# An attention and ternary-FFN kernel: scores issued one block ahead, half of a quantisation moved to ScalarE

## The chip, the cores and the metric

The kernel runs on all 8 cores of one Trainium2 chip, each core on one of the 8 sequences of the batch, with no exchange between them. The metric is the device time in microseconds of the slowest core. A core has TensorE (matmuls, results in PSUM), VectorE (DVE), ScalarE (ACT), GpSimd (POOL) and SyncE (SP); each works through its own queue in order and meets the others at semaphores. TensorE's clock is granted at one of two levels, 1.2 or 2.4 GHz; a granted clock of 0.67 over a stretch is a mean of 0.5 (1.2 GHz) and 1.0 (2.4 GHz).

## The reference

Per sequence (T = 2048 rows, C = 1024 columns, 16 heads of 64, hidden width 4096). What matters of it:

```
xn   = layernorm(x)
attn = softmax(q @ k.T / 8) @ v,  q, k, v = xn @ w{q,k,v}.T + b
y    = attn @ wo.T + bo
xq   = round(xn * 127/max|xn|) / (127/max|xn|)       # act_quant, per row
wq   = clip(round(w / mean|w|), -1, 1) * mean|w|     # weight_quant
h    = silu(depthwise_conv3(xq @ w1q.T) + conv_b)
out  = x + y + act_quant(h) @ w2q.T
```

Heads take 64 columns each; a key whose first input is 0 is masked.

## The kernel before

Five stages follow each other, written out as one queue per engine; nothing but the order of the code sets the order of the work.

**Layer norm (to about 240 us), L162 to L313.** 16 tiles of 128 rows. For each tile VectorE reduces, ScalarE squares (L217) and takes a square root (L226), VectorE normalises into `xn_t` (L279), casts to `xnb_t`, finds the maximum and quantises into `xqb_t`: L300 multiplies by the scale, L303 adds and subtracts `meff` (the constant that rounds), L306 multiplies back. TensorE transposes both (L185) through `psB`, and `evac` copies them to `xnT` and `xqT`. Between these, ScalarE streams the 64 chunks of the two FFN weights through `wf` to sum their absolute values: `wabs` (L206) frees a slot, `wdma` (L199) then issues the load of the chunk two ahead, so two loads of 512 KB are in flight.

**Projections (to about 316 us), L573.** q and k of the first pair of heads and v of the first four heads, from `xnT`, into `psD`, copied out by VectorE (L647, L653).

**Attention (316 to 1785 us), L576 to L595 and L605 to L624.** 8 pairs of heads, 4 blocks of 512 queries, 16 blocks of 128 keys: 512 blocks j. `scores(j)` (L564, L567, one head on each half of the rows) writes 1024 columns into half j%2 of `psA`. ScalarE takes the exponential into one of three slots of `probs` (L617). `emit_ctx(j)` (L537, L541) multiplies `probs` by v and accumulates in `psC`; its extra column of ones gives the denominators. After 16 blocks VectorE copies sums and denominators out (L683 to L687), TensorE spreads the denominators over partitions (L551, L553) and VectorE takes the reciprocal (L661) and scales. A second stream fills the gaps: the projections of the next heads, in halves of four matmuls, one half at every even block in the first six pairs of heads (q and k in the first 32 blocks, v in the other 32), at every fourth block in the seventh, none in the eighth. A third stream quantises the FFN weights: per 8 blocks one load (L380), two ScalarE operations (L387, L395), a clip on VectorE (L638) and a store (L413).

TensorE's queue goes by pairs of blocks: the context of the pair before, two projection slots, then the scores of both blocks. The first score of the pair waits until the exponentials of the pair before are done (L591), since they read the halves of `psA` that it writes.

**Output projection, L702 to L741.** GpSimd loads `wo_bf` over the memory of `xnT`, `wf`, `wqb`, `wblk` and `wvq` once these are free (its waits are L703 to L706); TensorE waits for that load at L716.

**FFN (to the end)**: first matmul, convolution, silu, row maximum, quantisation, second matmul, by blocks of 512 rows. The change does not touch it.

Of the kernel before, what the change touches and what calls it, by code (L numbers as in the profile page):

```python
# [11 lines left out]
AF = mybir.ActivationFunctionType  # L12
# [3 lines left out]
NT = T // 128  # L16
# [17 lines left out]
def _build():  # L34
# [24 lines left out]
    def sem(name):  # L59
        if name not in semn:  # L60
            semn[name] = E(nc.semaphore(name))
            cnt[name] = 0
        return semn[name]
# [51 lines left out]
    def on(engname, fn):  # L115
        getattr(blk, engname)(fn)
# [75 lines left out]
    def p1_scalar(s):  # L192
# [10 lines left out]
        def wabs(ch):  # L203
# [5 lines left out]
            inc("wabs")  # L209

        wdma(0); wdma(1)
        for i in range(NT):
            b = i % 2
# [7 lines left out]
            for ch in (4 * i, 4 * i + 1):  # L221
                wabs(ch)
                if ch + 2 < NW:
                    wdma(ch + 2)
            s.wait_ge(sem("p1v"), 18 * i + 5)
            s.activation(out=stt[:, b * 16 + 3:b * 16 + 4],  # L226
# [3 lines left out]
            for ch in (4 * i + 2, 4 * i + 3):  # L230
                wabs(ch)
                if ch + 2 < NW:
                    wdma(ch + 2)
    on("scalar", p1_scalar)

    def p1_vector(v):
# [14 lines left out]
        for i in range(NT):  # L251
# [25 lines left out]
            v.tensor_tensor(c(7), c(6), c(5), OP.mult).then_inc(sem("p1v"), 1); inc("p1v")  # L277
            v.wait_ge(sem("p1v"), val("p1v"))
            v.tensor_scalar(xnt, xt, c(1), c(7), OP.add, OP.mult).then_inc(  # L279
                sem(f"xf{b}"), 1)  # L280
# [4 lines left out]
            if i >= 2:  # L285
# [13 lines left out]
            v.wait_ge(sem("p1v"), val("p1v"))  # L299
            v.tensor_scalar(xnt, xnt, c(11), None, OP.mult).then_inc(sem("p1v"), 1); inc("p1v")  # L300
            v.wait_ge(sem("p1v"), val("p1v"))
            v.wait_ge(sem("p0v"), MEFF)
            v.tensor_scalar(xnt, xnt, meff[:, 0:1], meff[:, 0:1],  # L303
                            OP.add, OP.subtract).then_inc(sem("p1v"), 1); inc("p1v")
            v.wait_ge(sem("p1v"), val("p1v"))
            v.tensor_scalar(xqb_t[:, b * 1024:(b + 1) * 1024], xnt,  # L306
                            invsx[:, i:i + 1], None, OP.mult).then_inc(sem("p1xq"), 1); inc("p1xq")
            if i >= 1:
# [176 lines left out]
    def p23_tensor(t):  # L485
# [71 lines left out]

        def scores(j):
            it, kc = divmod(j, NT)
            hp, qb = divmod(it, NQB)  # L560
            pp = kc % 2
            sA = psA[:, pp * 1024:pp * 1024 + 512]
            sB = psA[:, pp * 1024 + 512:pp * 1024 + 1024]
            t.matmul(sA, kTv[0:64, hp % 2, kc * 128:(kc + 1) * 128],  # L564
                     qTv[0:64, hp % 2, qb * 512:(qb + 1) * 512],
# [5 lines left out]
            inc("p3s")  # L571

        for item in prods[:PROLOG]:  # L573
            prod_block(item)
        NJ3 = NHP * NQB * NT
        for pm in range(NJ3 // 2):  # L576
            j0 = 2 * pm
            it, kc = divmod(j0, NT)
            hp, qb = divmod(it, NQB)
            jl0 = j0 - hp * 64  # L580
            if jl0 == 0:
                t.wait_ge(sem("pde"), last_k[hp] + 1)
            if j0 >= 2:
                emit_ctx(j0 - 2)
                emit_ctx(j0 - 1)
            for item, half in seg_sched[hp].get(jl0, []):
                prod_block(item, half)
            for item, half in seg_sched[hp].get(jl0 + 1, []):
                prod_block(item, half)
            if j0 >= 2:  # L590
                t.wait_ge(sem("p3exp"), j0)  # L591
            scores(j0)
            scores(j0 + 1)
        emit_ctx(NJ3 - 2)
        emit_ctx(NJ3 - 1)  # L595
# [106 lines left out]
    def p35_gload(g):  # L702
        g.wait_ge(sem("p3pf"), P3PF)  # L703
        g.wait_ge(sem("wqv"), NW)
# [534 lines left out]
```

## Time and profile before

| what | us |
|---|---|
| median of 3 runs | 2784.5 (2782.46 to 2786.21) |
| profiled execution | 2784.95 |
| its span (slowest core, core 4) | 2783.3 |
| spans of the 8 cores | 2753.5 to 2783.3 |
| TensorE matmul busy | 1686.4 (61%) |
| ScalarE busy | 1118.1 (40%) |
| VectorE busy | 968.4 (35%) |
| GpSimd busy | 101.6 (4%) |

No engine is busy for most of the span. The busy time is a mean over stages with different limits, so each stage is read by itself: a table by stretches says where an engine is full and at which clock, and the timeline of a stretch says who waited for whom. In a timeline row the bracket at the end is the idle time of that engine just before the row, and what ended it. Matmuls overlap in their pipeline, so the distance between two starts tells more than the duration of one.

### The profile page before, as it was taken

The numbers are of one execution on the slowest core, as the hardware profiler recorded it, in microseconds if no ns is written. First come the engines' busy times: TensorE is split into PE (matmuls) and PEld (weight loads), VectorE is DVE, ScalarE is ACT, GpSimd is POOL, SyncE is SP. The second block draws the span as 40 slices with busy tenths as digits, with TensorE's granted clock in tenths as the row PEclk, the third lists the DMA queues.
The fourth block names the chain that finished last, engine by engine and source line by source line (L and its number), as shares of the span: only waits on it lengthen the run. The fifth ranks groups of instructions, "written<-read, shape, count | busy, mean of one in ns | idle before, by whom it ended". The sixth has DMA issues, their size and how long they took to land.

```text
span 2783.3 us, 24362 instructions; the slowest of 8 cores (2753.5 to 2783.3 us)
## 1 busy us (share of the span) xinstructions
PE 1686.4 (61%) x6887; PEld 571.6 (21%) x6986; DVE 968.4 (35%) x1392; ACT 1118.1 (40%) x1331; POOL 101.6 (4%) x193
## 2 busy tenths in 40 slices
PE   0114666666666666666666666398656666676666
PEld 0112211111111111111111111033323232232222
DVE  5674122221212121212112221213678258348423
ACT  3441244444444444443444455302356036126215
POOL 0000000000000000000000000000111001001000
PEclk9999576676665867767656655589888888888889
DMA  6754021111111111111100010201221422432344
GB/s 167 199 196 106 7 46 35 37 38 35 37 43 34 38 38 36 41 35 38 38 34 34 35 38 34 39 15 41 70 76 65 127 89 66 131 97 66 115 120 143
DMA packets 117954, 186.33 MB, mean 67 GB/s; under 512 B 44482, under 2 KB 77379, under 8 KB 117828
## 3 DMA queue, kind: packets, MB, share of 16 engines
q10 hardware_dynamic: 36864, 83.90, 10.0%
q0 software_dynamic: 16864, 50.35, 6.8%
q1 hardware_dynamic: 64100, 50.52, 6.1%
q8 instruction: 64, 1.05, 0.1%
q14 instruction: 62, 0.51, 0.1%
HBM read 167.95 MB, written 25.17 MB: 69 GB/s over the span
## 4 chain that ended last, share of the span: by engine, by line
PE 45%; ACT 17%; issue 13%; DMA 12%; DVE 11%; ACTq 1%; DVEq 0%; SPq 0%; POOL 0%; POOLq 0%
ACT probs L617 11%; PE psC L537 7%; PE psD L501 6%; DMA wf<-w_t 6%; PE psA L564 5%; PE psC L541 5%; PE psA L867 5%; PE psC L914 4%; PE psD L513 4%; DVE amax L1039 3%; ACT wf L387 3%; DMA w2q_sb<-w2q_stage 3%; PE psA L725 2%; PE psC L551 2%; DVE u_sb L1058 1%
## 5 line engine op out<-in xcount | busy, mean ns | idle before, releaser
L617 ACT ACTIVATE probs<-psA,bias_exp 128x1024 bf16<-128x1024 f32 x512 | 548.8, 1110 | 782.1 <-PE psA L567 782.0
L537 PE MATMUL psC<-probs,vroll 128*65 128x512 bf16 x512 | 256.5, 501 | 427.3 <-ACT probs L617 427.3
L867 PE MATMUL psA<-xqT,w1q_sb 128*128 128x512 bf16 x984 | 289.5, 440 | 159.6 <-DVE u_sb L1063 94.8
L541 PE MATMUL psC<-probs,vroll 128*65 128x512 bf16 x512 | 267.6, 523 | 0.0
L567 PE MATMUL psA<-qroll,kroll 64*128 64x512 bf16 x512 | 227.8, 540 | 0.0
L564 PE MATMUL psA<-qroll,kroll 64*128 64x512 bf16 x512 | 227.5, 539 | 0.0
L537 PEld LDWEIGHTS psC<-probs,vroll 128*65 128x65 bf16 x512 | 61.5, 120 | 778.7 <-issue 778.7
L914 PE MATMUL psC<-w2q_sb,hq 128*128 128x512 bf16 x561 | 162.7, 400 | 72.4 <-DMA w2q_sb<-w2q_stage 42.1
L501 PE MATMUL psD<-xnT,wblk 128*128 128x512 bf16 x480 | 185.2, 521 | 18.7 <-issue 5.6
L777 ACT ACTIVATE u_sb<-psA,cws 128x512 f32<-128x512 f32 x128 | 87.1, 681 | 262.8 <-PE psA L872 262.4
L799 ACT ACTIVATE qscr<-qscr,meff 128x512 f32<-128x512 f32 x128 | 91.5, 715 | 226.8 <-DVE qscr L1074 214.0
L647 DVE CAST vroll<-psD 128x256 bf16<-128x256 f32 x64 | 27.3, 427 | 439.1 <-PE psD L520 439.1
L867 PEld LDWEIGHTS psA<-xqT,w1q_sb 128*128 128x128 bf16 x1024 | 101.5, 107 | 285.2 <-issue 217.9
L513 PE MATMUL psD<-wvq,xnT 128*128 128x256 bf16 x512 | 121.8, 393 | 13.3 <-DVE vroll L647 12.2
L1058 DVE SCALAR_TENSOR_TENSOR u_sb<-psA,cws,u_sb 128x512 f32<-128x512 f32 x128 | 95.8, 749 | 90.8 <-ACT u_sb L777 90.8
L653 DVE TENSOR_SCALAR qroll<-psD,bqc 128x512 bf16<-128x512 f32 x32 | 24.0, 751 | 284.5 <-PE psD L501 284.5
L551 PE MATMUL psC<-denrow,onesr_s 1*64 1x512 f32 x64 | 60.2, 1042 | 96.5 <-DVE denrow L687 96.5
L185 PE MATMUL psB<-identb_s,xqb_t 128*128 128x128 bf16 x128 | 16.2, 307 | 168.9 <-DVE xnT L247 168.9
L653 DVE TENSOR_SCALAR kroll<-psD,bkc 128x512 bf16<-128x512 f32 x32 | 24.0, 751 | 266.0 <-PE psD L501 266.0
L661 DVE RECIPROCAL rtile<-psC 128x512 f32<-128x512 f32 x32 | 107.2, 3349 | 9.3 <-PE psC L553 9.2
L206 ACT ACTIVATE wf<-wf 128x1024 f32<-128x1024 f32 x64 | 67.6, 1056 | 99.9 <-DMA wf<-w_t 96.3
L1039 DVE TENSOR_REDUCE amax<-h_act 128x512 f32<-128x2048 f32 x28 | 102.9, 3676 | 5.7 <-ACT h_act L788 5.7
(139 smaller groups left out, 1999.3 us busy)
## 6 DMA issues: line engine op xcount, KB each, us to landing
wf<-w_t ACTq DMA_DIRECT2D x128, 512.0 KB, 4.1
w1q_sb<-w1q_stage POOLq DMA_DIRECT2D x128, 256.0 KB, 2.9
w2q_sb<-w2q_stage SPq DMA_DIRECT2D x128, 128.0 KB, 2.2
w2q_sb<-w2q_stage ACTq DMA_DIRECT2D x128, 128.0 KB, 2.2
x_t<-x SPq DMA_DIRECT2D x16, 512.0 KB, 7.2
w1q_stage<-wqb SPq DMA_DIRECT2D x32, 256.0 KB, 2.5
w2q_stage<-wqb SPq DMA_DIRECT2D x32, 256.0 KB, 2.0
xr_t<-x POOLq DMA_DIRECT2D x32, 256.0 KB, 3.8
```

The source lines that it names most:

```text
L501: mm = t.matmul(psD[:, 0:512], wblk[:, off + cc * 128:off + (cc + 1) * 128], xnTv[:, cc, b * 512:(b + 1) * 512], start=(cc == 0), stop=(cc ...
L513: t.matmul(psD[:, 0:256], xnTv[:, cc, ti * 128:(ti + 1) * 128], wvq[:, (qv % 2) * 2048 + cc * 256:(qv % 2) * 2048 + (cc + 1) * 256], start ...
L537: t.matmul(psC[0:65, 0:512], v_v[:, qvj % 2, kcj, laj, 0:65], probs[:, pslot * 1024:pslot * 1024 + 512], start=(kcj == 0), stop=(kcj == NT ...
L541: mm = t.matmul(psC[0:65, 512:1024], v_v[:, qvj % 2, kcj, laj + 1, 0:65], probs[:, pslot * 1024 + 512:pslot * 1024 + 1024], start=(kcj == ...
L551: t.matmul(psC[0:64, 1024:1536], onesr[0:1, 0:64], denrow[0:1, 0:512], start=True, stop=True)
L564: t.matmul(sA, kTv[0:64, hp % 2, kc * 128:(kc + 1) * 128], qTv[0:64, hp % 2, qb * 512:(qb + 1) * 512], start=True, stop=True, tile_positio ...
L567: mm = t.matmul(sB, kTv[64:128, hp % 2, kc * 128:(kc + 1) * 128], qTv[64:128, hp % 2, qb * 512:(qb + 1) * 512], start=True, stop=True, til ...
L617: s.activation(out=probs[:, pslot * 1024:(pslot + 1) * 1024], in_=psA[:, pp * 1024:(pp + 1) * 1024], func=AF.Exp, scale=0.125, bias=bias_e ...
L867: t.matmul(ps[:, 0:512], w1q_sb[:, b * 1024 + cc * 128:b * 1024 + (cc + 1) * 128], xqTv[:, cc, tb * 512:tb * 512 + 512], start=(cc == 0), ...
L914: mm = t.matmul(psm2, hq_v[:, jc, tt * 128:(tt + 1) * 128], w2q_sb[:, b2 * 512:(b2 + 1) * 512], start=(jc == 0), stop=(jc == NJC - 1))
L1039: v.reduce_max(amax2[:], hT[:, :, 4 * k:4 * k + 4], axis=AX, apply_absolute_value=True).then_inc(sem("p4fo"), 1)
L1058: v.scalar_tensor_tensor(u_sb[:, ub * 512:(ub + 1) * 512], ps[:, 1:513], cws[:, jc * 3 + 1:jc * 3 + 2], u_sb[:, ub * 512:(ub + 1) * 512], ...
```

## The change

Three edits, the instructions of which are otherwise the same.

**Attention.** TensorE's queue goes block by block: scores of block j, context of block j-1, the projection slot of block j. The wait for the exponential that frees the half of `psA` is now for block j-2 alone.

**Layer norm.** VectorE multiplies by the scale and adds `meff` in one operation (L300 and the addition of L303). The subtraction and the multiplication back become two ScalarE operations, in `quant_tail`, placed for tile i-1 after the second weight chunk of tile i and ahead of its square root; the last tile's stand at the end. VectorE's count of `p1v` per tile falls from 18 to 16.

**wo load.** Its wait for the last context matmul becomes one for the last q, k and v projections; the waits for the quantised weights and their stores stay.

```diff
+        def quant_tail(i2):
+            b2 = i2 % 2
+            xnt2 = xn_t[:, b2 * 1024:(b2 + 1) * 1024]
+            s.wait_ge(sem("p1q1"), i2 + 1)
+            s.activation(out=xnt2, in_=xnt2, func=AF.Identity,
+                         bias=meffneg[:, 0:1]).then_inc(sem("p1rt"), 1)
+            s.wait_ge(sem("p1rt"), val("p1rt"))
+            if i2 >= 2:
+                s.wait_ge(sem("p1tpm"), 2 * i2 - 2)
+            s.activation(out=xqb_t[:, b2 * 1024:(b2 + 1) * 1024], in_=xnt2,
+                         func=AF.Identity,
+                         scale=invsx[:, i2:i2 + 1]).then_inc(sem("p1xq"), 1)
...
+            if i >= 1:
+                quant_tail(i - 1)
+            s.wait_ge(sem("p1v"), 16 * i + 5)
-            s.wait_ge(sem("p1v"), 18 * i + 5)
...
+            if i >= 2:
+                v.wait_ge(sem("p1xq"), i - 1)
             v.tensor_scalar(xnt, xt, c(1), c(7), OP.add, OP.mult).then_inc(
...
-            v.tensor_scalar(xnt, xnt, c(11), None, OP.mult)
-            v.tensor_scalar(xnt, xnt, meff[:, 0:1], meff[:, 0:1],
-                            OP.add, OP.subtract)
-            v.tensor_scalar(xqb_t[:, b * 1024:(b + 1) * 1024], xnt,
-                            invsx[:, i:i + 1], None, OP.mult)
+            v.tensor_scalar(xnt, xnt, c(11), meff[:, 0:1],
+                            OP.mult, OP.add).then_inc(sem("p1q1"), 1)
...
-        for pm in range(NJ3 // 2):
-            j0 = 2 * pm
-            if j0 >= 2:
-                emit_ctx(j0 - 2)
-                emit_ctx(j0 - 1)
-            for item, half in seg_sched[hp].get(jl0, []): ...
-            for item, half in seg_sched[hp].get(jl0 + 1, []): ...
-            if j0 >= 2:
-                t.wait_ge(sem("p3exp"), j0)
-            scores(j0)
-            scores(j0 + 1)
+        for j in range(NJ3):
+            if j >= 2:
+                t.wait_ge(sem("p3exp"), j - 1)
+            scores of block j, as before
+            if j >= 1:
+                emit_ctx(j - 1)
+            for item, half in seg_sched[hp].get(jl, []):
+                prod_block(item, half)
...
     def p35_gload(g):
-        g.wait_ge(sem("p3pf"), P3PF)
+        g.wait_ge(sem("qkp"), 8 * NHP)
+        g.wait_ge(sem("vmm"), 4 * NT)
```

TensorE's queue before, at the end of the first 16 blocks. L564 and L567 are scores, L537 and L541 context, L551 and L553 the spread denominators, L501 a projection half:

```order
L564 MATMUL psA<-qroll,kroll 128x512 [waits p3exp]
L567 MATMUL psA<-qroll,kroll 128x512
L564 MATMUL psA<-qroll,kroll 128x512
L567 MATMUL psA<-qroll,kroll 128x512
L537 MATMUL psC<-probs,vroll 65x512 [waits p3exp,pde]
L541 MATMUL psC<-probs,vroll 65x512
L537 MATMUL psC<-probs,vroll 65x512 [waits p3exp,pde]
L541 MATMUL psC<-probs,vroll 65x512
L551 MATMUL psC<-denrow,onesr_s 64x512 [waits p3ev2]
L553 MATMUL psC<-denrow,onesr_s 64x512
L501 MATMUL psD<-xnT,wblk 128x512 [waits pde,lk]
L501 MATMUL psD<-xnT,wblk 128x512 x3
```

The same place after, where L588 and L591 are scores, L553 and L557 context, L567 and L569 the denominators and L517 the projection half:

```order
L588 MATMUL psA<-qroll,kroll 128x512 [waits p3exp]
L591 MATMUL psA<-qroll,kroll 128x512
L553 MATMUL psC<-probs,vroll 65x512 [waits p3exp,pde]
L557 MATMUL psC<-probs,vroll 65x512
L588 MATMUL psA<-qroll,kroll 128x512 [waits p3exp]
L591 MATMUL psA<-qroll,kroll 128x512
L553 MATMUL psC<-probs,vroll 65x512 [waits p3exp,pde]
L557 MATMUL psC<-probs,vroll 65x512
L567 MATMUL psC<-denrow,onesr_s 64x512 [waits p3ev2]
L569 MATMUL psC<-denrow,onesr_s 64x512
L517 MATMUL psD<-xnT,wblk 128x512 [waits pde,lk]
L517 MATMUL psD<-xnT,wblk 128x512 x3
```

One block's scores now stand between two blocks' contexts, so the scores of the first block of the next 16 are ahead of the last context and of the denominators; the projection half and the scores after it still stand behind the denominators.

ScalarE's queue in layer norm before, from the second weight chunk of a tile on (L206 weight chunk, L199 the load two ahead, L226 square root):

```order
L206 ACTIVATE wf,wsum<-wf 128x1024 [waits wl2]
L199 DMA wf<-w_t 128x1024 [waits wabs]
L226 ACTIVATE stt<-stt 128x1 [waits p1v]
L206 ACTIVATE wf,wsum<-wf 128x1024 [waits wl0]
L199 DMA wf<-w_t 128x1024 [waits wabs]
```

And after, where L244 is the square root and L215 and L221 are `quant_tail`:

```order
L206 ACTIVATE wf,wsum<-wf 128x1024 [waits wl2]
L199 DMA wf<-w_t 128x1024 [waits wabs]
L215 ACTIVATE xn_t<-xn_t,meffneg 128x1024 [waits p1q1]
L221 ACTIVATE xqb_t<-xn_t,invsx 128x1024 [waits p1rt]
L244 ACTIVATE stt<-stt 128x1 [waits p1v]
L206 ACTIVATE wf,wsum<-wf 128x1024 [waits wl0]
L199 DMA wf<-w_t 128x1024 [waits wabs]
```

Two operations of 128x1024 now stand ahead of the square root and of the third weight chunk of each tile but the first.

## Rows read from the trace of the kernel before

**Rows 1.** The page's costliest groups; count, busy us, mean ns, idle before and releaser.
```profile
L617 ACT ACTIVATE probs<-psA,bias_exp 128x1024 bf16<-128x1024 f32 x512 | 548.8, 1110 | 782.1 <-PE psA L567 782.0
...
L537 PE MATMUL psC<-probs,vroll 128*65 128x512 bf16 x512 | 256.5, 501 | 427.3 <-ACT probs L617 427.3
...
L661 DVE RECIPROCAL rtile<-psC 128x512 f32<-128x512 f32 x32 | 107.2, 3349 | 9.3 <-PE psC L553 9.2
```

**Rows 2.** Stretches: length, PE, PEld, DVE, ACT, POOL busy, clock, DMA share, GB/s.
```profile
0.00:240.00 240.00, 33.17 (x263) 25.54 (x263) 152.30 (x381) 96.24 (x177) 2.85 (x9) 1.00 0.62 176
...
316.00:1785.00 1469.00, 939.08 (x3021) 237.90 (x3048) 306.62 (x325) 682.27 (x641) 7.41 (x14) 0.67 0.13 36
...
1800.00:2000.00 200.00, 156.48 (x709) 61.42 (x725) 79.46 (x91) 32.44 (x49) 13.48 (x26) 0.88 0.17 45
```

**Rows 3.** Timeline, last pair of heads, 1.2 GHz; start, duration, engine, line, idle before.
```profile
1757.54 0.60 PE L564 MATMUL psA<-qroll,kroll 64*128 64x512 bf16 x1
...
1758.30 2.12 ACT L617 ACTIVATE probs<-psA,bias_exp 128x1024 bf16<-128x1024 f32 x2 [1.98 <-PE psA L567]
...
1759.67 0.60 PE L537 MATMUL psC<-probs,vroll 128*65 128x512 bf16 x1 [1.09 <-ACT probs L617]
...
1760.67 0.61 PE L537 MATMUL psC<-probs,vroll 128*65 128x512 bf16 x1
...
1761.64 0.60 PE L564 MATMUL psA<-qroll,kroll 64*128 64x512 bf16 x1
```

**Rows 4.** Timeline, a pair with half a k product, 2.4 GHz.
```profile
568.43 2.12 ACT L617 ACTIVATE probs<-psA,bias_exp 128x1024 bf16<-128x1024 f32 x2 [3.55 <-PE psA L567]
...
570.80 0.38 PE L537 MATMUL psC<-probs,vroll 128*65 128x512 bf16 x1 [0.41 <-ACT probs L617]
...
572.18 0.39 PE L564 MATMUL psA<-qroll,kroll 64*128 64x512 bf16 x1
...
572.73 1.11 ACT L617 ACTIVATE probs<-psA,bias_exp 128x1024 bf16<-128x1024 f32 x1 [1.15 <-PE psA L567]
```

**Rows 5.** Timeline, TensorE, 1.2 GHz: with half a v, and half a k product.
```profile
447.90 0.61 PE L537 MATMUL psC<-probs,vroll 128*65 128x512 bf16 x1
...
450.04 0.60 PE L564 MATMUL psA<-qroll,kroll 64*128 64x512 bf16 x1
...
565.13 0.61 PE L537 MATMUL psC<-probs,vroll 128*65 128x512 bf16 x1 [1.54 <-ACT probs L617]
...
567.80 0.46 PE L564 MATMUL psA<-qroll,kroll 64*128 64x512 bf16 x1
```

**Rows 6.** Timeline, the accumulators emptied after 16 blocks, 1.2 GHz.
```profile
1741.92 0.61 PE L537 MATMUL psC<-probs,vroll 128*65 128x512 bf16 x1
...
1744.84 1.22 DVE L687 COPY denrow<-psC 1x1024 f32<-1x1024 f32 x1
...
1746.31 1.08 PE L551 MATMUL psC<-denrow,onesr_s 1*64 1x512 f32 x1 [3.36 <-DVE denrow L687]
...
1748.21 0.60 PE L564 MATMUL psA<-qroll,kroll 64*128 64x512 bf16 x1
```

**Rows 7.** Layer norm: waits to 215 us, then timeline of one tile.
```profile
ACT wf L206 <- DMA wf<-w_t: 92.5, 51, 3.9
...
197.38 0.20 ACT L226 ACTIVATE stt<-stt 128x1 f32<-128x1 f32 x1 [0.51 <-DVE stt L267]
...
199.15 1.06 ACT L206 ACTIVATE wf<-wf 128x1024 f32<-128x1024 f32 x1 [1.57 <-DMA wf<-w_t]
...
204.66 0.75 DVE L306 TENSOR_SCALAR xqb_t<-xn_t,invsx 128x1024 bf16<-128x1024 f32 x1
```

**Rows 8.** Groups in attention, shapes apart; count, busy us, mean ns.
```profile
L395 ACT ACTIVATE wf<-wf,meffneg 128x1024 f32<-128x1024 f32 x64 | 73.3, 1146 | 0.0
```

**Rows 9.** Timeline after the last exponential, GpSimd.
```profile
1794.73 4.23 POOL L708 DMA_DIRECT2D wo_bf<-wo_t  x8 [447.45 <-DMA w2q_stage<-wqb]
```

**Rows 10.** Line 617: duration in ns, least, median and most; first and last start.
```profile
L617 ACT ACTIVATE probs<-psA,bias_exp x512: 1100/1112/1116, 317.6 to 1779.5; 128x1024 bf16<-128x1024 f32 x171
```

More of the change, by code:

```diff
@@ L209, in wabs @@
             inc("wabs")
+        def quant_tail(i2):
[4 more added lines that the diff above has]
+                         bias=meffneg[:, 0:1]).then_inc(sem("p1rt"), 1)
+            inc("p1rt")
+            s.wait_ge(sem("p1rt"), val("p1rt"))
[4 more added lines that the diff above has]
+                         scale=invsx[:, i2:i2 + 1]).then_inc(sem("p1xq"), 1)
+            inc("p1xq")
         wdma(0); wdma(1)
+        s.wait_ge(sem("p0v"), MEFF)
         for i in range(NT):
@@ L233, in p1_scalar @@
                     wdma(ch + 2)
+        quant_tail(NT - 1)
     on("scalar", p1_scalar)
@@ L299, in p1_vector @@
             v.wait_ge(sem("p1v"), val("p1v"))
-            v.tensor_scalar(xnt, xnt, c(11), None, OP.mult).then_inc(sem("p1v"), 1); inc("p1v")
-            v.wait_ge(sem("p1v"), val("p1v"))
             v.wait_ge(sem("p0v"), MEFF)
-            v.tensor_scalar(xnt, xnt, meff[:, 0:1], meff[:, 0:1],
-                            OP.add, OP.subtract).then_inc(sem("p1v"), 1); inc("p1v")
-            v.wait_ge(sem("p1v"), val("p1v"))
-            v.tensor_scalar(xqb_t[:, b * 1024:(b + 1) * 1024], xnt,
-                            invsx[:, i:i + 1], None, OP.mult).then_inc(sem("p1xq"), 1); inc("p1xq")
+            v.tensor_scalar(xnt, xnt, c(11), meff[:, 0:1],
+                            OP.mult, OP.add).then_inc(sem("p1q1"), 1); inc("p1q1")
             if i >= 1:
@@ L556, in emit_ctx @@
                 inc("p3nb")
-        def scores(j):
+        for item in prods[:PROLOG]:
+            prod_block(item)
+        NJ3 = NHP * NQB * NT
+        for j in range(NJ3):
             it, kc = divmod(j, NT)
             hp, qb = divmod(it, NQB)
+            jl = j - hp * 64
+            if jl == 0:
+                t.wait_ge(sem("pde"), last_k[hp] + 1)
             pp = kc % 2
@@ L571, in scores @@
             inc("p3s")
-        for item in prods[:PROLOG]:
-            prod_block(item)
-        NJ3 = NHP * NQB * NT
-        for pm in range(NJ3 // 2):
-            j0 = 2 * pm
[L578 to L582, printed above, removed]
-            if j0 >= 2:
-                emit_ctx(j0 - 2)
-                emit_ctx(j0 - 1)
-            for item, half in seg_sched[hp].get(jl0, []):
-                prod_block(item, half)
-            for item, half in seg_sched[hp].get(jl0 + 1, []):
-                prod_block(item, half)
-            if j0 >= 2:
-                t.wait_ge(sem("p3exp"), j0)
-            scores(j0)
-            scores(j0 + 1)
-        emit_ctx(NJ3 - 2)
+            if j >= 1:
+                emit_ctx(j - 1)
+            for item, half in seg_sched[hp].get(jl, []):
+                prod_block(item, half)
         emit_ctx(NJ3 - 1)
```

## The prediction, made before the changed kernel was run

> **What bounds the kernel now.** I read the page first, then the busy times by stretch, then the timeline inside each stretch that the change touches. The profiled execution took 2784.95 us (span 2783.3 us and 1.7 us around it) and stands 0.45 us over the median of 2784.5 us, so the sum is made against 2785. About 0.2% (6 us) is what a measurement of this kernel can tell from no change.
>
> The page shows the exponentials as the largest ScalarE group, 548.8 us busy, with 782 us of idle time before them that ends with a score matmul on TensorE; TensorE in turn waits 427 us for exponentials ahead of L537 [rows 1]. Two engines that wait for each other are a handoff, not a full engine. The stretches say where: attention runs from 316 to 1785 us, 1469 us, with TensorE 64% and ScalarE 46% busy, at a granted clock of 0.67 [rows 2]. That share is a mean over 1.2 and 2.4 GHz.
>
> The timeline shows the handoff, at 1.2 GHz and with no projection work: scores start at 1757.54, their exponential at 1758.30 (0.76 later), the first context matmul at 1759.67 (1.37 later), the second exponential's context matmul at 1760.67, and only 0.97 after that the next scores, at 1761.64. The pair lasts 4.10 [rows 3]. ScalarE idles from the end of a pair's second exponential until new scores exist: two exponentials take 2.12 of it.
>
> **The change: attention (L558 to L595).** Before, both slots of psA are filled, both emptied, both used, and then filled again. After, the scores of block j stand ahead of the context of block j-1, so ScalarE has a slot to work on while TensorE does context, projection and the next scores. No instruction is added or removed here, only moved. The ring that remains runs from one exponential to the one two blocks on, in the same slot: exponential to its context matmul, context (and a projection piece) to the scores, scores to the exponential. For two blocks:
> - at 1.2 GHz, no projection: 1.37 + 0.97 + 0.76 = 3.10 (before 4.10) [rows 3];
> - at 1.2 GHz with a half q/k product: context to scores is 2.67 [rows 5], so 1.37 + 2.67 + 0.76 = 4.80;
> - at 1.2 GHz with a half v product: 2.14 with its bias matmul [rows 5], some 0.3 less in the half without; mean ring 4.1;
> - at 2.4 GHz with a half q/k product: 1.37 + 1.38 + 0.55 = 3.30, where the same pair takes 4.30 before [rows 4];
> - at 2.4 GHz with a half v product: half of the cold 1.0 that it adds onto the ring without one, 2.45: 3.0;
> - at 2.4 GHz, none: 1.37 + 0.53 + 0.55 = 2.45 (1.38 less 0.85, half of what the product adds cold, 2.67 - 0.97). ScalarE is the limit here: per eight blocks eight exponentials of 1.06 and two weight operations of 1.15 [rows 3, 8], 10.8, or 2.7 a pair; I take 2.75, and 3.2 for the cold case.
>
> A product half stands at every even block, so it always lies in one and the same ring: that ring sets the pace, the other has slack. The weight operations (L387, L395) fall into ScalarE's slack of over 1 us in the rings with a product; before, L387 stood between a pair's exponentials and cost 1.13 every fourth pair, 0.28 a pair.
>
> Every 16 blocks the accumulators are emptied. Last context matmuls at 1741.92, VectorE's last copy at 1744.84, broadcast at 1746.31, scores at 1748.21: 6.29 where a usual handoff has 0.97, so 5.3 extra [rows 6]. That chain is not shortened: the broadcast still stands ahead of the next projection piece and scores. One exponential now runs under it, no more. At 2.4 GHz half of the broadcast's 1.9 and of the context's 0.8 goes: 4.4 extra.
>
> Groups of 16 blocks (8 pairs): 12 with q/k, 12 with v, 4 of the seventh head pair (product in every other pair), 4 with none. All at 1.2 GHz: 12 x 43.7 + 12 x 38.1 + 4 x 37.3 + 4 x 30.9 = 1254. All at 2.4 GHz: 12 x 30.8 + 12 x 28.4 + 4 x 28.6 + 4 x 26.4 = 930. The same working for the order of before gives 1580 and 1242; at a granted 0.67 a third of the time is at 2.4 GHz, 1 / (0.34/1242 + 0.66/1580) = 1446 against 1469 in the trace: 1.6% too little, and I add that below.
>
> **The clock.** Bounds are the two levels throughout. TensorE is busy 64% of attention now at a granted 0.67 [rows 2]. The same work of a q/k pair that took 4.30 stands in 3.30, so TensorE idles less by 1 us a pair. The stretch with the same or more work per us is the output projection and first FFN block, 78% busy at a granted 0.88 [rows 2]. I take 0.88, since the emptying still leaves a gap of some 4 us every 16 blocks, after which the clock was at 1.2 GHz here [rows 6]. Three quarters at 2.4 GHz: 1 / (0.76/930 + 0.24/1254) = 991, plus 1.6% = 1007. **1469 to 1007: 462 us less.**
>
> The Trainium skill, page TensorE: Matmul & The Clock Gate, section "A second HAM failure mode: psum-queue depth-cycling", says that a matmul loop which cycles through PSUM slots with short idles between groups keeps dropping and regaining its clock. That rule speaks against my 0.88, for the new loop still has such idles; the trace so far agrees for the old loop (0.67). What it would give is worked out as rival 1.
>
> **The change: layer norm (L192 to L307).** VectorE loses two of three passes over 128x1024 (0.75 each [rows 7], with their waits 1.8 per tile). It is not the pace: it is busy 152 of the 240 us [rows 2], while ScalarE streams the FFN weights with two loads in flight and waited 92.5 us for them in 51 places [rows 7]. VectorE's new wait, for the quantised copy of tile i-2 before `xn_t` is written again, has a whole tile (some 13 us) of room, so nothing queues behind it. ScalarE gains two passes for 15 tiles ahead of the square root: by the nearest rows 1.15 each plus a wait on itself [rows 8], 2.5 in all. Queued behind them are the square root (VectorE waits for it), the next weight pass and its load. In the trace ScalarE idled 1.57 between square root (197.38) and weight pass (199.15) [rows 7]; so 2.5 less 1.6 is 0.9 late per tile, and part of that returns at the next pass, whose load was issued before. Bounds: -2 (the last tile's VectorE tail alone) to +38 (15 x 2.5, none hidden); 14 tiles x 0.9 is 13. I take **+5**, near the lower rows because the next pass has idle time too.
>
> **The change: wo load (L702).** Its wait for the last context matmul becomes a wait for the last projections. In the trace the load started at 1794.73, released by the last store of the quantised weights [rows 9], 15 us after the last exponential at 1779.5 [rows 10]; the clip ahead of that store stays behind the last normalisation on VectorE. **0**; bounds 0 and, if that store came early, 15 less.
>
> Sum: 2785 - 462 + 5 + 0 = 2328.
>
> **Rivals.**
> 1. The clock stays at 0.67 because the short waits remain. 1 / (0.34/930 + 0.66/1254) x 1.016 = 1139, 330 less: 2460. For it: VectorE, ScalarE and TensorE still meet at each block. Against it: stretches with fewer waits had 0.88. Chance 0.13; the page's rule above is this one. Down to 1.2 GHz throughout would be 1274, so 2595: chance 0.03.
> 2. The clock stays at 2.4 GHz nearly throughout: 930 x 1.016 = 945: 2266. Against it the gap at each emptying. Chance 0.10.
> 3. Slower: scores into one half of psA do not proceed while ScalarE reads the other half. Then each block is a full serial handoff, 3.1 cold and 2.45 warm, plus the products: per pair 7.9 with q/k cold, 5.7 warm. Summed as above 2029 and 1533, at 0.67 1828: 359 more, 3149. It decides once exponentials start over 2.9 us apart (1469/512). Against it: a pair's second scores already ran beside its first exponential, and all 512 took 1100 to 1116 ns [rows 1, 10]. Chance 0.03.
> 4. The loop gains nothing because something else limits each block to 2.9 us, say VectorE's 3.35 us reciprocal [rows 1], which stands ahead of a product's copy out of psD: 2790. Against it: that product ends two pairs after the reciprocal starts, 6.6 us even at 3.30 a pair. Chance 0.01.
>
> **How the numbers follow.** Forecast 0.70, with its own range 2290 to 2385 (clock 0.93 to 0.80; layer norm -2 to +13); rivals as above. The range for 8 in 10 reaches to rival 2's and most of rival 1's side: 2258 to 2450. Faster 0.96, same 0.01, slower 0.03.
>
> **What would show it.** Right: idle before the exponentials falls from 782 us to about 320; exponentials 1.65 apart with q/k; attention some 1007 us; granted clock in it 0.85 or more; scores of block j start beside the exponential of j-1; the gap ahead of each broadcast as before. Layer norm ends within 13 us of before with VectorE 1.8 us per tile less busy. The wo load starts 15 us after the last exponential, as now. Wrong: a clock near 0.67 (rival 1), score matmuls that start only at an exponential's end (rival 3), or layer norm over 15 us longer.

## The result, and the profile after

The changed kernel takes 2316.4 us (median of 8 runs, 2309.4 to 2328.6) against 2784.1 us for the kernel before beside it: a ratio of 0.832, 95% interval 0.8305 to 0.8341, or 468 us less. 2328 was forecast, with 2258 to 2450 as the range. In the profiled execution of the kernel called e11 below, cores 4 to 7 spent 235 to 259 us at a granted clock of 0.81, a level between the two, and another of its four runs was slow as a whole, so its median leaves that run out and its attention time is that of cores 0 to 3.

Where the time went can be read from the stages of both traces, as the median of the 8 cores. From the first to the last exponential: 1458 us before, 995 us after, 463 less. The last copy of layer norm starts at 234.9 us before and 229.2 us after. From the start of the last exponential to the first output projection: 29.9 and 29.4 us. From the output projection's start to the end: 964 and 962 us. The time saved is attention's, almost alone.

The costliest groups of the page of the changed kernel, which answer to [rows 1]: L622 is the exponential, L553 the first context matmul.

```profile
L622 ACT ACTIVATE probs<-psA,bias_exp 128x1024 bf16<-128x1024 f32 x512 | 556.0, 1111 | 312.6 <-PE psA L591 306.7
...
L553 PE MATMUL psC<-probs,vroll 128*65 128x512 bf16 x512 | 214.3, 419 | 166.2 <-ACT probs L622 158.5
```

The exponentials cost what they did (1111 ns each). The idle time ahead of them fell from 782 to 313 us, and TensorE's ahead of L553 from 427 to 166: the handoff shrank on both sides. By stretch (as [rows 2]; layer norm and attention):

```profile
0.00:240.00 240.00, 34.02 (x266) 26.29 (x266) 128.15 (x349) 129.76 (x209) 2.96 (x9) 1.00 0.59 176
318.00:1315.00 997.00, 737.48 (x3047) 222.08 (x3045) 303.89 (x322) 684.37 (x641) 7.39 (x14) 0.88 0.18 53
```

TensorE is busy 737 us of 997 in attention where it was busy 939 of 1469: the same matmuls took less time, since the granted clock is 0.88 (0.887 as the median of the 8 cores) and was 0.67. ScalarE does the same 684 us of work and is busy 69% of the stage.

The timeline of some blocks at 2.4 GHz with half a k product in each second one (answers to [rows 4]); L588 scores, L517 the product:

```profile
605.83 0.39 PE L588 MATMUL psA<-qroll,kroll 64*128 64x512 bf16 x1
...
606.70 0.39 PE L588 MATMUL psA<-qroll,kroll 64*128 64x512 bf16 x1
...
607.39 1.11 ACT L622 ACTIVATE probs<-psA,bias_exp 128x1024 bf16<-128x1024 f32 x1
...
607.74 0.38 PE L553 MATMUL psC<-probs,vroll 128*65 128x512 bf16 x1 [0.65 <-ACT probs L622]
...
608.17 1.02 PE L517 MATMUL psD<-xnT,wblk 128*128 128x512 bf16 x4
...
609.13 0.39 PE L588 MATMUL psA<-qroll,kroll 64*128 64x512 bf16 x1
```

From the scores at 605.83 to those two blocks on at 609.13 it is 3.30 us, and 3.30 is also the median of all rings with half a q/k product at 2.4 GHz over the 8 cores, with a weight operation in them or without. The scores at 606.70 were done before the exponential at 607.39 began, so ScalarE had work in `psA` while TensorE did the context at 607.74 and the product at 608.17. Between 607.74 and 609.13 lie context and product, 1.39 us, the 1.38 of [rows 4]. In the last pair of heads, without products, scores two blocks apart start 2.47 apart (answers to [rows 3]):

```profile
1274.82 0.39 PE L588 MATMUL psA<-qroll,kroll 64*128 64x512 bf16 x1
...
1277.29 0.39 PE L588 MATMUL psA<-qroll,kroll 64*128 64x512 bf16 x1
```

The accumulators' emptying (answers to [rows 6]); L692 is VectorE's last copy, L567 the broadcast:

```profile
595.70 0.38 PE L553 MATMUL psC<-probs,vroll 128*65 128x512 bf16 x1 [0.34 <-ACT probs L622]
...
597.83 1.22 DVE L692 COPY denrow<-psC 1x1024 f32<-1x1024 f32 x1
...
599.30 0.61 PE L567 MATMUL psC<-denrow,onesr_s 1*64 1x512 f32 x1 [3.01 <-DVE denrow L692]
...
600.49 1.89 PE L517 MATMUL psD<-xnT,wblk 128*128 128x512 bf16 x4
...
602.31 0.60 PE L588 MATMUL psA<-qroll,kroll 64*128 64x512 bf16 x1
```

From the last context to the scores: 6.61 us, with the product of 1.8 in it. TensorE waits 3.01 us of them for the copies. The context at 595.70 ran at 2.4 GHz (0.38 us); the product after the wait at 1.2 GHz (1.89 for four, where 608.17 shows such a product at the high level with 0.96 to the next scores).

Layer norm, ScalarE's queue for one tile and VectorE's wait (answers to [rows 7]); L215 and L221 are the moved passes, L244 the square root:

```profile
196.61 1.15 ACT L215 ACTIVATE xn_t<-xn_t,meffneg 128x1024 f32<-128x1024 f32 x1 [0.51 <-ACT wf L206]
197.90 1.15 ACT L221 ACTIVATE xqb_t<-xn_t,invsx 128x1024 bf16<-128x1024 f32 x1
198.96 0.19 ACT L244 ACTIVATE stt<-stt 128x1 f32<-128x1 f32 x1
199.05 1.04 ACT L206 ACTIVATE wf<-wf 128x1024 f32<-128x1024 f32 x1
199.25 0.16 DVE L288 RECIPROCAL stt<-stt 128x1 f32<-128x1 f32 x1 [3.25 <-ACT stt L244]
```

```profile
ACT wf L206 <- DMA wf<-w_t: 61.9, 37, 4.9
DVE stt L288 <- ACT stt L244: 45.4, 15, 7.2
```

The two passes of 1.15 stand where ScalarE waited for a weight chunk: that wait sums to 61.9 us and was 92.5. VectorE now waits 45.4 us for square roots, and is busy 128 us of the first 240 where it was 152.

The load of wo, and the exponentials' least, median and longest ns with first and last start (answer to [rows 9, 10]):

```profile
1328.88 4.23 POOL L714 DMA_DIRECT2D wo_bf<-wo_t  x8 [323.54 <-DMA w2q_stage<-wqb]
```

```profile
L622 ACT ACTIVATE probs<-psA,bias_exp x512: 1101/1114/1120, 318.6 to 1314.5; 128x1024 bf16<-128x1024 f32 x171
```

The load is released by the last store, as before, 14.4 us after the start of the last exponential (15.2 before).

### The profile page after: what moved, and what is told of

It reads as the page before. It is cut to its first block, busy times and chain, and to the rows that moved or that the text cites. A ratio compares the mean times of both kernels' runs of the same rounds, so it can differ in the third digit from the quotient of the medians.

```text
span 2307.9 us, 24746 instructions; the slowest of 8 cores (2288.5 to 2307.9 us)
## 1 busy us (share of the span) xinstructions
PE 1492.8 (65%) x6986; PEld 555.7 (24%) x6986; DVE 944.0 (41%) x1360; ACT 1155.5 (50%) x1363; POOL 101.3 (4%) x193
## 4 chain that ended last, share of the span: by engine, by line
PE 42%; ACT 18%; DVE 14%; DMA 12%; issue 11%; ACTq 1%; DVEq 0%; SPq 0%; POOL 0%; POOLq 0%
ACT probs L622 10%; PE psA L873 6%; DMA wf<-w_t 6%; PE psC L920 5%; PE psD L517 5%; PE psC L553 5%; PE psA L588 4%; DVE amax L1045 4%; PE psC L557 3%; DMA w2q_sb<-w2q_stage 3%; PE psD L529 3%; PE psA L731 3%; PE psC L567 2%; ACT wf L206 2%; ACT wf L403 2%
## 5 line engine op out<-in xcount | busy, mean ns | idle before, releaser
L622 ACT ACTIVATE probs<-psA,bias_exp 128x1024 bf16<-128x1024 f32 x512 | 556.0, 1111 | 312.6 <-PE psA L591 306.7
L553 PE MATMUL psC<-probs,vroll 128*65 128x512 bf16 x512 | 214.3, 419 | 166.2 <-ACT probs L622 158.5
L591 PE MATMUL psA<-qroll,kroll 64*128 64x512 bf16 x512 | 215.5, 421 | 0.0
L588 PE MATMUL psA<-qroll,kroll 64*128 64x512 bf16 x512 | 215.3, 421 | 0.0
L920 PE MATMUL psC<-w2q_sb,hq 128*128 128x512 bf16 x576 | 168.0, 403 | 69.6 <-DMA w2q_sb<-w2q_stage 40.0
L557 PE MATMUL psC<-probs,vroll 128*65 128x512 bf16 x512 | 210.7, 411 | 0.0
L517 PE MATMUL psD<-xnT,wblk 128*128 128x512 bf16 x512 | 148.8, 421 | 11.2 <-DVE qroll L658 4.5
L553 PEld LDWEIGHTS psC<-probs,vroll 128*65 128x65 bf16 x512 | 56.9, 111 | 312.8 <-issue 312.8
L1064 DVE SCALAR_TENSOR_TENSOR u_sb<-psA,cws,u_sb 128x512 f32<-128x512 f32 x128 | 95.8, 748 | 86.3 <-ACT u_sb L783 80.3
L567 PE MATMUL psC<-denrow,onesr_s 1*64 1x512 f32 x64 | 54.5, 947 | 96.8 <-DVE denrow L692 96.8
L1014 DVE TENSOR_TENSOR out_t<-xr_t,y_attn 128x512 f32<-128x512 f32 x32 | 22.0, 688 | 223.7 <-PE psD L920 196.0
L529 PE MATMUL psD<-wvq,xnT 128*128 128x256 bf16 x512 | 95.7, 328 | 13.3 <-DVE vroll L652 12.2
L1080 DVE TENSOR_TENSOR qscr<-h_act,shb_sb 128x512 f32<-128x512 f32 x128 | 87.5, 684 | 39.1 <-ACT qscr L805 38.5
L1069 DVE SCALAR_TENSOR_TENSOR u_sb<-psA,cws,u_sb 128x512 f32<-128x512 f32 x128 | 96.0, 750 | 13.3
```

What stands on the lines that cost most here:

```text
L517: mm = t.matmul(psD[:, 0:512], wblk[:, off + cc * 128:off + (cc + 1) * 128], xnTv[:, cc, b * 512:(b + 1) * 512], start=(cc == 0), stop=(cc ...
L529: t.matmul(psD[:, 0:256], xnTv[:, cc, ti * 128:(ti + 1) * 128], wvq[:, (qv % 2) * 2048 + cc * 256:(qv % 2) * 2048 + (cc + 1) * 256], start ...
L553: t.matmul(psC[0:65, 0:512], v_v[:, qvj % 2, kcj, laj, 0:65], probs[:, pslot * 1024:pslot * 1024 + 512], start=(kcj == 0), stop=(kcj == NT ...
L557: mm = t.matmul(psC[0:65, 512:1024], v_v[:, qvj % 2, kcj, laj + 1, 0:65], probs[:, pslot * 1024 + 512:pslot * 1024 + 1024], start=(kcj == ...
L567: t.matmul(psC[0:64, 1024:1536], onesr[0:1, 0:64], denrow[0:1, 0:512], start=True, stop=True)
L588: t.matmul(sA, kTv[0:64, hp % 2, kc * 128:(kc + 1) * 128], qTv[0:64, hp % 2, qb * 512:(qb + 1) * 512], start=True, stop=True, tile_positio ...
```

## The experiments

All were timed against the kernel before; the last column is the time from first to last exponential in one profiled execution, median of 8 cores (e11: of cores 0 to 3).

| kernel | median us | ratio to before, 95% interval | attention us |
|---|---|---|---|
| changed kernel | 2316.4 | 0.832 [0.8305, 0.8341] | 995 |
| e1 attention edit alone | 2318.3 | 0.834 [0.8315, 0.8367] | 997 |
| e2 layer norm edit alone | 2778.8 | 0.999 [0.9972, 1.0008] | 1450 |
| e3 wo edit alone | 2778.8 | 0.999 [0.9975, 1.0014] | 1460 |
| e4 before, two ScalarE passes more | 2786.8 | 1.0025 [1.0006, 1.0043] | 1453 |
| e5 before, matmuls that add zero | 2643.2 | 0.948 [0.9456, 0.9499] | 1317 |
| e6 changed, products in quarters | 2297.4 | 0.825 [0.8223, 0.8273] | 971 |
| e7 changed, late broadcast | 2268.5 | 0.814 [0.8121, 0.8155] | 945 |
| e8 before, VectorE's passes fewer | 2782.2 | 0.998 [0.9970, 0.9996] | 1454 |
| e9 changed, early last clip | 2302.5 | 0.8275 [0.8250, 0.8300] | 995 |
| e10 changed, product ahead of context | 2252.3 | 0.8095 [0.8078, 0.8111] | 927 |
| e11 e7 + e9 + e10 | 2236.8 | 0.8036 [0.8005, 0.8067] | 920 |
| e12 e11 in quarters | 2194.9 | 0.788 [0.7865, 0.7901] | 881 |

### Which edit carries the gain (e1, e2, e3)

Each edit of the diff put alone into the kernel before.

> The attention edit alone. Ring theory (the two-block ring of exponential, context, projection piece and scores sets the pace): the whole of the gain is here, 460 to 468 us, so about 2320; attention about 996 us at a granted clock of 0.88 as in the changed kernel. If the layer norm or the wo edit carried part of it, this run stays over 2322.

> The layer norm edit alone. Theory A (the FFN weight stream sets the pace; ScalarE's added passes fill its idle time; only the last tile's VectorE tail gets shorter): 0 to 2 us less, 2782 to 2784. Theory B (VectorE set part of the pace): 5 us less or more. The working of the prediction (added passes delay the next load by 0.9 per tile, part returned): 5 us more.

> The wo edit alone. Last store of the quantised weights releases the load: 0, within 2 us of 2784. If the last context matmul had been a gate: 10 to 15 us less.

The attention edit alone gives 0.834 where all three give 0.832, intervals overlapping. It carries the gain. The layer norm edit alone is 3 us less, from 8 less to 2 more: the 5 more of the prediction lie outside, theories A and B both inside. The wo edit alone is the same as before.

### What of it is the clock, what the order (e5)

```diff
+        def filler(kc, n):
+            if kc == 0:
+                return
+            for f in range(n):
+                t.matmul(psC[0:65, (f % 2) * 512:(f % 2) * 512 + 512], zw[:, 0:65],
+                         xnTv[:, f % 8, 0:512], start=False, stop=False)
...
+                filler((j0 - 2) % NT, 4)
                 emit_ctx(j0 - 2)
+                filler((j0 - 1) % NT, 1)
                 emit_ctx(j0 - 1)
```

> The order of before, with five more context matmuls per pair of blocks that add zero (a stationary tile of zeros) placed where TensorE waits for the exponentials, so that the clock rises and the handoff stays. Ring theory: at a granted clock of about 0.9 the old order needs (0.8/1242 + 0.2/1580)^-1 x 1.016 = 1318 us of attention, so 140 us less than before, about 2640; the other 320 us of the gain are the order's own. Rival (the gain is the clock's: the new order only keeps TensorE busier): attention near 1000 us, about 2320.

It took 2643 us, and attention 1317 (median), where 2640 and 1318 were expected. The stretch of attention (columns as in rows 2):

```profile
316.00:1635.00 1319.00, 999.82 (x4147) 321.07 (x4188) 305.28 (x324) 678.86 (x639) 7.38 (x14) 0.89 0.15 40
```

The granted clock is the changed kernel's (0.887 in both as the median of the 8 cores, from first to last exponential). With it the old order still needs 1317 us, and the new one 995. So of the 463 us, 141 are what the clock alone gives the old order, and 322 the order's at the clock that both have. The timeline shows the handoff left as it was, two pairs with half a v product each, 3.91 and 4.09 us apart (L630 exponential, L533 the matmuls that add zero):

```profile
629.12 2.12 ACT L630 ACTIVATE probs<-psA,bias_exp 128x1024 bf16<-128x1024 f32 x2 [0.93 <-PE psA L578]
...
633.01 1.05 PE L533 MATMUL psC<-xnT,zw 128*65 128x512 bf16 x4
633.03 2.12 ACT L630 ACTIVATE probs<-psA,bias_exp 128x1024 bf16<-128x1024 f32 x2 [1.79 <-PE psA L578]
...
637.12 1.11 ACT L630 ACTIVATE probs<-psA,bias_exp 128x1024 bf16<-128x1024 f32 x1 [1.97 <-PE psA L578]
```

Pairs with half a q/k product at 2.4 GHz and without a weight operation are 4.30 us apart here and 4.31 in the kernel before (medians over the 8 cores), so the added matmuls did not lengthen the handoff. The rival that the new order only keeps TensorE busier is out. In the changed kernel the higher clock came with the new order, without any added work.

### What sets the pace of the ring (e6, e10)

In e6 a product has four parts of two matmuls, one at each block:

```diff
-        chunks = [(item, half) for item in seg_prod[hp] for half in (0, 1)]
+        chunks = [(item, half) for item in seg_prod[hp] for half in (0, 1, 2, 3)]
...
-            ccs = range(NCH) if half is None else range(half * 4, half * 4 + 4)
+            ccs = range(NCH) if half is None else range(half * 2, half * 2 + 2)
```

> The changed kernel with the projections cut into quarters of two matmuls, one at every block, in place of halves of four at every even block. Ring theory: a projection half lies in one ring and that ring sets the pace (3.30 us a pair at 2.4 GHz with q/k); shared by both rings it is 2.9, and with v 2.75 in place of 3.0: 12 x 8 x 0.4 + 12 x 8 x 0.25 = 62 us less than the changed kernel, about 2255. Rival (TensorE's total work or ScalarE sets the pace): no change, 2316.

A third of it came: attention 24 us less, the kernel 19 to 21, where 62 were expected. Four blocks' scores (L589) and what came between (L623 exponential, L411 a weight operation, L554 context):

```profile
600.87 0.39 PE L589 MATMUL psA<-qroll,kroll 64*128 64x512 bf16 x1
...
602.18 0.39 PE L589 MATMUL psA<-qroll,kroll 64*128 64x512 bf16 x1
...
602.43 1.14 ACT L411 ACTIVATE wf<-wf,meffneg 128x1024 f32<-128x1024 f32 x1
...
603.74 0.39 PE L589 MATMUL psA<-qroll,kroll 64*128 64x512 bf16 x1
...
604.83 0.38 PE L554 MATMUL psC<-probs,vroll 128*65 128x512 bf16 x1 [0.69 <-ACT probs L623]
...
605.78 0.39 PE L589 MATMUL psA<-qroll,kroll 64*128 64x512 bf16 x1
```

From 600.87 to 603.74 it is 2.87, the 2.9 expected. Then a weight operation of 1.14 stands ahead of an exponential, the context waits for it at 604.83, and the next step is 2.04 long instead of 1.4. In the ring of 3.30 such an operation hid in ScalarE's slack; in one of 2.87 part of it does not. I had let it vanish in both. Over the 8 cores most q/k rings of e6 at 2.4 GHz are 2.9 long or, by where the weight operation falls, 3.4 to 3.7, and their mean is 3.29 against 3.33 in the changed kernel. The ring theory's number for an undisturbed pair is right, the sum over pairs was not. The gain did not come where it was expected either: per group of 16 blocks the q/k groups became 0.8 us shorter, the v groups 0.2, and those of the seventh pair of heads, which the expectation left out, 3.0, which over their four groups is half of the 24 us.

e10 leaves the halves whole and moves them ahead of the context:

```diff
+            for item, half in seg_sched[hp].get(jl, []):
+                prod_block(item, half)
             if j >= 1:
                 emit_ctx(j - 1)
-            for item, half in seg_sched[hp].get(jl, []):
-                prod_block(item, half)
```

> The changed kernel with the projection half ahead of the context matmuls of its block, where TensorE waits for an exponential, in place of behind them. Ring theory: the projection leaves the ring, which is then 2.45 us a pair at 2.4 GHz for every kind, so ScalarE's 2.75 sets the pace: 12 x 8 x (3.30 - 2.75) + 12 x 8 x (3.0 - 2.75) = 77 us less, about 2240. Rival (TensorE's total work sets the pace): no change, 2316.

It took 2252, attention 68 us less for 77 expected. By groups, about 31 us of the 68 are the q/k groups' (53 expected), 23 the v groups' (24 expected), and 14 the seventh pair's, which the expectation left out. Products and exponentials side by side (columns as before):

```profile
602.10 1.11 ACT L622 ACTIVATE probs<-psA,bias_exp 128x1024 bf16<-128x1024 f32 x1 [0.32 <-PE psA L591]
...
602.88 1.04 PE L517 MATMUL psD<-xnT,wblk 128*128 128x512 bf16 x4
603.11 1.14 ACT L411 ACTIVATE wf<-wf,meffneg 128x1024 f32<-128x1024 f32 x1
...
603.75 0.38 PE L553 MATMUL psC<-probs,vroll 128*65 128x512 bf16 x1
...
604.15 2.11 ACT L622 ACTIVATE probs<-psA,bias_exp 128x1024 bf16<-128x1024 f32 x2
...
604.28 0.39 PE L588 MATMUL psA<-qroll,kroll 64*128 64x512 bf16 x1
...
605.51 0.38 PE L553 MATMUL psC<-probs,vroll 128*65 128x512 bf16 x1 [0.83 <-ACT probs L622]
```

The distance from context to scores is 0.53 (603.75 to 604.28), that of the ring without product. The product is not quite free: the exponential that the context at 603.75 needs ended at 603.21, and the row names no wait, so the product of 602.88 still held it up by some tenths. ScalarE's chain of weight operation (603.11) and exponential (604.15) is what the next context, at 605.51, waits for. The rival, that TensorE's total work sets the pace, is out for this order.

### The emptying chain (e7)

The two broadcast matmuls leave `emit_ctx` for a function of their own:

```diff
-            if kcj == NT - 1:
-                t.wait_ge(sem("p3ev2"), 3 * itj + 3)
...
             if j >= 1:
                 emit_ctx(j - 1)
+                if j >= NT + 2 and (j - 2) % NT == 0:
+                    bcast((j - 2) // NT - 1)
```

> The changed kernel with the denominators' broadcast taken out of the emptying chain: it stands behind the second context of the next 16 blocks, so the scores of the next block no longer wait for VectorE's three copies and the broadcast. Theory (the emptying chain costs 4.4 to 5.3 us in each of 32 groups, because scores stand behind it): about 2 us stay (the context waits for the copies), so 2 to 3 us less each, 65 to 95 us less, about 2235. Rival (the stall is the copies' own and only moves from the scores to the context): under 20 us less.

It took 2268 where 2235 was expected, attention 50 us less, 1.6 per group where 2 to 3 were expected. The timeline says what stayed (L696 the last copy, L568 the broadcast, L529 half a v product, L626 exponential):

```profile
613.59 0.38 PE L553 MATMUL psC<-probs,vroll 128*65 128x512 bf16 x1 [0.35 <-ACT probs L626]
...
615.10 1.11 ACT L626 ACTIVATE probs<-psA,bias_exp 128x1024 bf16<-128x1024 f32 x1 [0.59 <-PE psA L592]
...
617.30 0.38 PE L553 MATMUL psC<-probs,vroll 128*65 128x512 bf16 x1 [2.35 <-DVE denrow L696]
...
618.37 1.11 ACT L626 ACTIVATE probs<-psA,bias_exp 128x1024 bf16<-128x1024 f32 x1 [2.16 <-PE psA L592]
...
618.94 1.11 PE L568 MATMUL psC<-denrow,onesr_s 1*64 1x512 f32 x1
...
620.84 1.03 PE L529 MATMUL psD<-wvq,xnT 128*128 128x256 bf16 x4
```

The scores no longer wait, and one more exponential runs (615.10). The next context waits 3.7 us after the last one for the copies. After that wait the clock fell: the broadcast takes 1.9 us (618.94 to 620.84) and the product with its bias 1.3, both at 1.2 GHz, and both now lie in the ring. One stall became two smaller ones.

### Layer norm, its two halves (e4, e8)

e4 adds to the kernel before two Identity passes on a scratch slot of `wf`, ahead of the square root. e8 writes the quantised tile by one VectorE operation; it leaves out the rounding's subtraction and the multiplication back, on ScalarE too, so it computes other values and serves for its time alone.

```diff
+            if i >= 1:
+                dummy()          # e4: two passes of 128x1024 on ScalarE
             s.wait_ge(sem("p1v"), 18 * i + 5)
```

```diff
-            v.tensor_scalar(xnt, xnt, c(11), None, OP.mult)
-            v.tensor_scalar(xnt, xnt, meff[:, 0:1], meff[:, 0:1], OP.add, OP.subtract)
-            v.tensor_scalar(xqb_t[...], xnt, invsx[:, i:i + 1], None, OP.mult)
+            v.tensor_scalar(xqb_t[...], xnt, c(11), meff[:, 0:1], OP.mult, OP.add)
```

> The kernel before with two passes of 128x1024 added to ScalarE at the place of the new ones (on a scratch slot, their result unused), and VectorE's work left as it was. Theory A: the passes are hidden in the waits for weights, but the square root comes 2.5 us later and VectorE has less than 1 us of room per tile, so it becomes the pace: 14 tiles by 1 to 2 us, 14 to 28 us more. If VectorE has more room than that: 0 to 5 us more.

> The kernel before with VectorE's part of the layer norm edit alone: one operation writes the quantised tile, and the rounding's subtraction and the multiplication back are left out, on ScalarE too. Theory A (the weight stream sets the pace): 0 to 3 us less than before. Theory B (VectorE was part of the pace, and the new kernel gave that gain back on ScalarE): 6 us less or more.

The passes alone cost 7 us (2 to 12), the relief alone gives 5 (1 to 8), which lies between the 0 to 3 of theory A and the 6 of theory B. The edit has both: 3 less, within 8 less to 2 more, so the sum of the two, 2 more, is at its edge. The waits of e4 in the first 215 us:

```profile
ACT wf L206 <- DMA wf<-w_t: 62.9, 35, 5.3
DVE stt L286 <- ACT stt L241: 24.6, 15, 6.4
```

15 pairs of passes are 35 us of ScalarE work, and the waits for weights fell by 30 (92.5 to 62.9): most of it is hidden by the weight stream, as theory A has it. VectorE waits 24.6 us for square roots in e4 and 21.9 in the kernel before, so 14 to 28 us, my number if VectorE had under 1 us of room a tile, was too much. In e8 that wait is 38.2 us: most of what VectorE is relieved of turns into waiting, and some 5 us into time. In one execution the end of layer norm differs by 4 to 13 us between the 8 cores (223 to 243 us over these kernels), so the timed ratios bear the few us, not the traces.

### After attention (e9)

```diff
+            if j == NJ3 - 1:
+                wclip(NW - 1)
             if kc == NT - 1:
                 v.wait_ge(sem("p3pf"), (it + 1) * NT)
...
         ctx_norm(NHP * NQB - 1)
-        wclip(NW - 1)
```

> The changed kernel with the last weight chunk clipped ahead of the last copies out of the accumulators, so that its store no longer stands behind the last reciprocal. Theory (the last store alone releases the wo load, 14.4 us after the last exponential): the load starts within 3 us of the last exponential, the output projection then waits for the load and no longer for that store: 11 us less than the changed kernel, about 2305. If another wait took over at once: 0.

It took 2302, 13 less by the ratios (11 expected). The load of wo starts 2.6 us after the start of the last exponential (8 cores alike) and was 14.4, and the output projection starts 10 us earlier:

```profile
1310.78 2.11 ACT L622 ACTIVATE probs<-psA,bias_exp 128x1024 bf16<-128x1024 f32 x2
...
1314.36 4.23 POOL L715 DMA_DIRECT2D wo_bf<-wo_t  x8 [309.67 <-DMA w2q_stage<-wqb]
```

The first row holds the last two exponentials, the second of them from about 1311.8. The GpSimd load still names the store as its releaser; the store is earlier, since the clip no longer waits for the last normalisation. Only with this earlier clip (e9, e11, e12) can the wo edit matter, since the load of the kernel before also waits for the last context matmul. The clip without the wo edit was not tried.

### Together (e11, e12)

> The last two edits with the late broadcast (48 us less when alone): they touch different waits, so the gains add: 2316 - 77 - 48 - 11 = 2180. If the late broadcast only pays while the ring has slack, up to 30 us more.

> As the run before, with the projections in quarters at every block. Ring theory: the ring holds no projection any more and ScalarE sets the pace, so the finer cut gives nothing: within 10 us of the run before, either side.

Both expectations fell. e11 took 2237 where 2180, or up to 30 more, was expected: its attention (920) is 7 us under e10's (927), so the late broadcast, worth 50 alone, gave little on top of the earlier product. e12 took 2195, 42 us less than e11 (attention 881), where I expected a difference of at most 10. It is 0.788 of before, and 5% under the changed kernel. In e12 (L569 the broadcast, L590 scores, L554 context):

```profile
599.40 1.11 PE L569 MATMUL psC<-denrow,onesr_s 1*64 1x512 f32 x1
...
603.70 0.60 PE L590 MATMUL psA<-qroll,kroll 64*128 64x512 bf16 x1
...
604.64 0.63 PE L554 MATMUL psC<-probs,vroll 128*65 128x512 bf16 x1
...
605.64 0.61 PE L590 MATMUL psA<-qroll,kroll 64*128 64x512 bf16 x1
```

After the broadcast, still at 1.2 GHz (scores of 0.60), blocks follow each other at 1.94 (603.70 to 605.64), and the context row at 604.64 names no wait. A half of four matmuls would make every second one of them some 0.9 longer (an estimate: two matmuls more, where four took 1.8 at 1.2 GHz above). With halves TensorE's work per block is uneven, and only one finished half of `psA` stands between it and ScalarE; that, and the low clock after each emptying, would make the finer cut pay and the late broadcast not. This reading is argued from rows and was not tested by a run of its own. The traces add two things. Over a third of e12's gain on e11 is in the seventh pair of heads (27.4 us a group for 31.2). And e12 lost the clock less often: in the first six pairs of heads 69 of its 184 emptyings, with waits of 2.2 to 2.5 us, were not followed by 1.2 GHz, in e11 24 of 92 (cores 0 to 3), in e10 none of 184. What stays open is the share of each.

## Why the prediction was right, point by point

**The stage and the handoff.** Right. Attention carries the gain (e1), and the mechanism is the ring: 3.30 us for two blocks with a q/k product at 2.4 GHz, and 2.47 without one (2.45 was worked out), were read in the trace.

**The sum over groups.** 463 us less in attention for 462 forecast. Part of that exactness is luck: the 32 groups hide misses of both signs. At the forecast clock the sum has 33.7 us for a q/k group, 30.7 for v, 30.8 for one of the seventh pair of heads and 27.8 for one of the last; the means over the 8 cores are 32.0, 30.4, 33.1 and 29.0. In the groups without product I took ScalarE's 2.75 as the limit, the trace has rings of 2.47 broken by weight operations; e6 shows that these operations are not free as soon as the ring is short. The last two pairs of heads also ran at a lower clock (0.82 to 0.85 over the cores) than the first six (0.90 to 0.91), where the sum takes one clock for all.

**The clock.** 0.88 forecast and measured. It was taken from one other stretch with similar density, which was a choice, not a calculation; e5, with the same formula for the old order, gave 1317 for 1318; that was forecast for a clock of 0.9, and for the 0.887 that it had the formula gives 1326, so it is borne out between its two ends to within 1%. Rival 1, the clock at 0.67, did not come. The Trainium skill's rule behind it (TensorE: Matmul & The Clock Gate, "A second HAM failure mode: psum-queue depth-cycling") is not contradicted: short idles of 0.4 to 1.2 us remain, and a clock of 0.88 is not 1. But in the first six pairs of heads the traces put every fall of the clock (184 over the 8 cores) at an emptying, a wait of 3 us for VectorE, and none at the short waits between blocks. In the last two pairs, where products are few or none, 42 of 85 falls do lie between blocks, where the waits are 0.5 to 1.1 us, as the rule has it.

**The emptying.** Right in kind, the broadcast still ahead of the scores; 6.61 less a product of 1.8 is 4.8, just under the bracket of 4.95 (2.4 GHz) to 6.3 (1.2 GHz). What the sum left out is that the clock falls at the wait each time, so the product behind it runs at 1.2 GHz also where the blocks around it run at 2.4.

**Layer norm.** The term of the sum that was missed: +5 forecast, -3 (-8 to +2) measured (e2). The failed step is "VectorE is not the pace". It is near it: with the passes alone on ScalarE the kernel is 7 us slower (e4; 2 to 12), which bears out the +5 as the cost of the passes, and VectorE's relief alone is 5 us faster (e8; 1 to 8). I counted what the delay of the square root costs and not what the shorter VectorE chain gives back on all tiles.

**wo load.** Right: 0 (e3), released by the last store, which e9 shows by moving it.

**Rivals 2, 3 and 4.** Exponentials of 1101 to 1120 ns and scores that run beside them exclude the third; 3.30 a pair, the fourth; 0.88, the second. The third's 1828 us leaves out the 1.6% that the other sums have; with it the rival would stand at about 3178 us, and the conclusion is the same.

## What to carry to other kernels

When two engines wait for each other, write down the ring (from one operation to the same one a buffer turn later) with distances between starts, at each clock level, and put everything that need not be in it outside: issuing the producer one block ahead took 322 us off at an equal clock here, and moving an independent matmul group from behind to ahead of the wait another 64 off the kernel. Test a clock story by work that adds zero: it separates "busier" from "better ordered" in one run. What is hidden in slack must be priced again when an edit removes the slack, and gains that were measured alone need not add.

## What the runs showed of the hardware

Matmuls with a stationary tile of zeros raised the granted clock: 0.67 to 0.89 over attention (e5). In the changed kernel each wait of about 3.0 us at an emptying in the first six pairs of heads (184 over the 8 cores) stood between matmuls at 2.4 GHz ahead of it and matmuls at 1.2 GHz behind it, while the waits of 0.3 to 1.2 us between the blocks there were not followed by a fall; in the last two pairs, with few or no products, falls followed such short waits too (42 over the 8 cores). Exponentials of 128x1024 out of PSUM took 1101 to 1120 ns in the changed kernel, where TensorE writes the other half of `psA` beside many of them, and 1100 to 1116 before.
